# Routed experts on one core: where VectorE computes the remainders of the next block's weights

## The reference, cut to what matters

```python
logits = x @ gate_weight.T
scores = softmax(logits, axis=-1)
topk_w, topk_idx = top_k(scores, 2)
combine = zeros((T, E)).at[arange(T)[:, None], topk_idx].add(topk_w)
gu = einsum('th,efh->tef', x, gate_up_weights)      # E = 8, F = 352, H = 512
act = silu(gu[..., :F]) * gu[..., F:]
y = einsum('tef,te,ehf->th', act, combine, down_weights)
```

## Time and profile before

| | |
|---|---|
| time, median of 3 runs | 2822.68 us (2808.33, 2822.68, 2824.14) |
| the profiled execution's own time | 2808.16 us |
| its span | 2806.4 us |
| busy: PE, PEld | 2506.0 us (89%), 1464.9 us (52%) |
| busy: DVE, ACT, POOL | 1851.2 us (66%), 1257.6 us (45%), 1384.7 us (49%) |
| share of the chain that ended last | PE 52%, DVE 18%, POOL 10% |

### The profile page before, as it was taken

How to read it: one execution, slowest core, us unless ns; L and a number is a source line. 1 busy time by engine, 2 the same in 40 slices (tenths; PEclk the granted TensorE clock), 3 DMA queues, 4 the chain that set the end, 5 groups by cost and what they waited for, 6 DMA issues and landing times.

```text
span 2806.4 us, 33198 instructions
## 1 busy us (share of the span) xinstructions
PE 2506.0 (89%) x11722; PEld 1464.9 (52%) x11786; DVE 1851.2 (66%) x2240; ACT 1257.6 (45%) x1997; POOL 1384.7 (49%) x741
## 2 busy tenths in 40 slices
PE   5998949999999999989578799988988999999998
PEld 2454524444577888855233233333333333687776
DVE  4677875554565666556689789788978898722223
ACT  3443205541223666433557655763665443234333
POOL 0221338870050000330499999899999996122221
PEclk9999859998999999999899999999999999999999
DMA  6443583432053777531275676677576675100000
GB/s 222 139 120 101 78 120 87 95 86 113 12 226 133 261 260 261 197 116 51 94 196 153 179 203 176 162 192 205 168 196 195 166 209 194 57 0 16 15 1 30
DMA packets 278967, 384.98 MB, mean 137 GB/s; under 512 B 127104, under 2 KB 148608, under 8 KB 271392
## 3 DMA queue, kind: packets, MB, share of 16 engines
q1 hardware_dynamic: 268944, 335.77, 41.1%
q0 software_dynamic: 9296, 38.80, 5.6%
q10 hardware_dynamic: 576, 8.39, 0.7%
HBM read 312.91 MB, written 59.51 MB: 133 GB/s over the span
## 4 chain that ended last, share of the span: by engine, by line
PE 52%; DVE 18%; POOL 10%; issue 7%; ACT 5%; SPq 5%; DMA 3%; PEldq 0%; DVEq 0%; ACTq 0%; POOLq 0%; PEld 0%
PE psum L2037 7%; POOL arena L786 5%; PE psum L2215 4%; PE psum L2216 4%; POOL arena L792 4%; PE psum L1984 4%; SPq L2291 3%; DVE psum L1567 3%; DVE arena L1567 2%; PE psum L3017 2%; PE psum L2830 2%; PE psum L2188 2%; PE psum L2189 2%; DVE arena L2601 2%; PE psum L483 2%
## 5 line engine op out<-in xcount | busy, mean ns | idle before, releaser
L786 POOL TENSOR_TENSOR arena<-arena 128x1024 f32<-128x1024 f32 x256 | 625.8, 2453 | 137.8 <-DVE arena L1552 81.1
L2037 PE MATMUL psum<-arena,cst 128*128 128x512 f32 x1024 | 511.0, 638 | 118.5 <-POOL arena L792 87.2
L1090 ACT ACTIVATE psum<-arena,negA 128x512 f32<-128x512 f32 x512 | 333.3, 682 | 273.0 <-DVE arena L1567 234.1
L2037 PEld LDWEIGHTS psum<-arena,cst 128*128 128x128 f32 x1024 | 193.8, 201 | 422.4 <-issue 201.7
L1567 DVE TENSOR_TENSOR_SCAN arena<-psum,arena 128x512 f32<-128x512 f32 x256 | 310.7, 1213 | 101.3 <-ACT psum L1090 74.1
L1567 DVE TENSOR_TENSOR_SCAN psum<-psum,arena 128x512 f32<-128x512 f32 x256 | 297.9, 1209 | 37.3 <-POOL arena L786 36.4
L792 POOL TENSOR_TENSOR arena<-arena 128x1024 f32<-128x1024 f32 x128 | 308.0, 2407 | 10.9 <-DVE arena L1567 10.7
L840 POOL TENSOR_TENSOR arena<-arena 128x512 f32<-128x512 f32 x64 | 92.3, 1442 | 324.4 <-ACT arena L1215 299.4
L1984 PE MATMUL psum<-arena 128*128 128x512 f32 x512 | 230.3, 593 | 1.3 <-PE psum L1984 0.8
L2379 POOL TENSOR_TENSOR arena<-arena,cst 128x512 f32<-128x512 f32 x64 | 76.9, 1228 | 275.9 <-DVE arena L2683 191.4
L2367 POOL TENSOR_TENSOR arena<-arena,cst 128x1024 f32<-128x1024 f32 x96 | 184.7, 1952 | 43.0 <-PE psum L2931 25.7
(11 more groups left out here) (373 smaller groups left out, 4976.5 us busy)
## 6 DMA issues: line engine op xcount, KB each, us to landing
arena<-bc_scr SPq DMA_DIRECT2D x256, 512.0 KB, 5.5
arena<-w_exp SPq DMA_DIRECT2D x23, 1408.0 KB, 6.2
arena<-in_gu SPq DMA_DIRECT2D x48, 512.0 KB, 5.4
arena<-in_inw SPq DMA_DIRECT2D x32, 512.0 KB, 3.7
arena<-in_dn SPq DMA_DIRECT2D x31, 512.0 KB, 6.9
x_scr<-arena SPq DMA_DIRECT2D x19, 512.0 KB, 5.9
arena<-in_x SPq DMA_DIRECT2D x8, 1024.0 KB, 11.7
w_exp<-in_gu SPq DMA_DIRECT2D x16, 512.0 KB, 7.1
```

Of the source, the lines that this page charges most:

```text
L786: nc.gpsimd.tensor_tensor(dB[:, k % 4], du[:, j:j + 2], BC[:, k % RING, 0].unsqueeze(1).broadcast_to([P, 2, T]), ALU.mult).then_inc(s["db_ ...
L1090: nc.scalar.activation(psum[:, bank], dt[:, b % 2, j + t], ACT.Exp, scale=negA2[:, at:at + 1]).then_inc(s["da_ok"], 1)
L2037: ins = mm(psum[:, t], ident, dB[:, k % 4, t], start=False, stop=(n == NS - 1), skip_group_check=True)
```

## The change

`pieces(h)` now gives two lists, cut after the first `EARLY[h % 5]` pieces: two where h mod 5 = 0, otherwise one.

- VectorE: in front of `act_lo(h-1)` it does only the first list. The second list moves behind `tokens_lo(h+1)`; where h mod 5 = 4 it stays between `act_lo` and `act_b`.
- ScalarE: nothing changes but where h mod 5 = 3. There (3g+2, 2) moves from in front of `silu_b` to behind `act_hi`, and (3g+2, 3) from behind `act_hi` to behind `tokens_hi`.
- h = 0 stays as it was.

```diff
@@ ScalarE
-                if h:
-                    for k, j in pieces(h)[:-1]:
-                        hi(k, j)
+                first, then = pieces(h)
+                for k, j in first:
+                    hi(k, j)
                 silu_b(h)
                 if h:
                     act_hi(h - 1)
-                    for k, j in pieces(h)[-1:]:
+                    for k, j in then[:1]:
                         hi(k, j)
...
                     tokens_hi(h + 1)
-                if h == 0:
-                    for k, j in pieces(h):
-                        hi(k, j)
+                for k, j in then[1 if h else 0:]:
+                    hi(k, j)
                 if h:
                     rows_out(h - 1)
@@ VectorE
             for h in range(NH):
+                first, then = pieces(h)
+                for k, j in first:
+                    lo(k, j)
                 if h:
-                    for k, j in pieces(h)[:-1]:
-                        lo(k, j)
                     act_lo(h - 1)
-                    for k, j in pieces(h)[-1:]:
+                if h % 5 == 4:
+                    for k, j in then:
                         lo(k, j)
                 act_b(h)
                 if h + 1 < NH:
                     tokens_lo(h + 1)
-                if h == 0:
-                    for k, j in pieces(h):
+                if h % 5 != 4:
+                    for k, j in then:
                         lo(k, j)
@@ pieces
+        EARLY = (2, 1, 1, 1, 1)
+
         def pieces(h):
 
             at = [(3 * (h // 5) + k, j) for k, j in PIECE_AT[h % 5]]
-            return [(k, j) for k, j in at if 0 < k < NBLK]
+            cut = EARLY[h % 5] if h else 0
+            return [[(k, j) for k, j in part if 0 < k < NBLK] for part in (at[:cut], at[cut:])]
```

## The result

The changed kernel takes 2809.02 us in the median of 20 runs (2788.75 to 2822.12), the kernel before 2818.37 us in the median of its 20 runs beside them. The ratio is 0.997, with a 95% interval of 0.9956 to 0.9985; it leaves out one run of the kernel before, of 3673.78 us. That is about 8.5 us less (4.2 to 12.4), and the interval does not hold 1. The forecast was 7.8 us less and a median of 2814.9 us, in a range of 2797 to 2824.

What follows compares the result with a forecast made beforehand. TensorE was taken to set the pace, so only its pauses could be won: 5.6 us (gate) + 3.4 (down) - 1.2 (late load) = 7.8 us less, 2822.7 - 7.8 = 2814.9 us, range 2797 to 2824.

Steps and rivals of the forecast that it cites:

- What bounds the stage: Loop over the halves: TensorE, busy 34.43 of 35.00 us, sets the pace; only its pauses can be won.
- the ceiling of 21.6 us: TensorE's weight-load waits, 13.3 us at gate for `tokens_lo` and 8.3 at down for `act_lo`: the most to win.
- The price of a pause: On TensorE, a gate pause costs 0.40 us and a down pause 0.48, less at gate than the weight load's wait suggests.
- The sum of the parts: Over the loop: 5.6 us of gate pauses plus 3.4 of down pauses, less 1.2 for the load, gives 7.8 less.
- 14 x 0.40 = 5.6 us: Gate pauses at h mod 5 = 1 and 3 go when VectorE's last pieces move behind `tokens_lo`: 5.6 us won.
- 7 x 0.48 = 3.4 us: Seven down pauses at h mod 5 = 3 go, with one piece instead of two before `act_lo`: 3.4 us won.
- The cover of the moved pieces: VectorE's idle time before its next first piece, 2.70 us in the row, hides a moved piece, so `act_lo` is not delayed.
- The late load: Block 3g+4's load, issued later, makes ScalarE wait some 1.2 us in iteration 0, seven times: 1.2 us lost in all.
- by the sum: In iterations 0 and 1, with landing time L, ScalarE waits L - 6.52 us and a period loses L - 7.53.
- Slower by the late load: Rival: at a landing of 11.2 us, block 3g+4's load makes the kernel 17 us slower, 2839.7 us; chance 0.05.
- Nothing: Rival: the waits are a symptom of TensorE's own pace and the gaps stay, 2822.7 us; chance 0.07.
- most of it comes back: Rival: gate pauses at h mod 5 = 1 and iteration 3's late `act_lo` return; gain 2.8 us, 2819.9; chance 0.10.

Runs made afterwards that it cites:

- iteration 0 alone: Kernel before, with only VectorE's last piece of iteration 0 moved behind the tokens; loop from h = 3 took 252.7 us, against 255.5 before.
- iteration 3 as before: Changed kernel with the old order restored on both engines where h mod 5 = 3; loop from h = 3 took 252.9 us, against 247.5 changed.
- iteration 2 alone: Kernel before, with only VectorE's last piece of iteration 2 moved behind the tokens; loop from h = 3 took 255.8 us, against 255.5 before.
- iteration 3 alone: Kernel before, with the new order only where h mod 5 = 3, on both engines; loop from h = 3 took 256.0 us, against 255.5 before.
- the load still later: Changed kernel, with SyncE issuing block 3g+4's load only after VectorE's piece (3g+3, 0) too; loop from h = 3 took 265.7 us, against 247.5.

## Why the prediction was right, and where its steps were not

*What bounds the stage: right.* TensorE sets the pace, and with all its pauses gone the loop is shorter by 11.4 us from h = 3, within the ceiling of 21.6 us. Of the rest, 6.7 us are three waits that stay: 3.5 and 1.6 in the first halves, and 1.6 at the last down of the loop. The remaining 3.5 us are mostly waits that overstate their pause.

*The price of a pause: right.* 0.40 us at gate: iteration 0 alone brought 2.8 us in seven periods. The rule that an undisturbed weight load is early and a waiting load overstates the pause holds.

*The sum of the parts: right in total, wrong in how it is split.* The step that failed is "14 x 0.40 = 5.6 us" beside "7 x 0.48 = 3.4 us", as if the seven pauses at gate of 3 and the seven at down of 3 were separate. They are one delay. ScalarE's two pieces begin behind `rows_out`, which begins 0.43 us behind down's last matmul, whether gate has paused or not. `act_lo` is therefore ready at a fixed distance from the last down, and a gate that starts earlier only meets a longer pause at down. The same three places in the kernel before (last down, `act_lo`, first down of iteration 3, the last in the earlier trace rows too):

```profile
938.43 0.40 PE L1909 MATMUL psum<-r 96*128 96x512 f32 x1
```

```profile
943.43 0.55 DVE L1413 TENSOR_TENSOR r<-psum,r 128x384 fp32r<-128x384 f32 x1
```

`act_lo` ends 5.55 us behind that last down and down starts 5.61 behind it (944.04), with a gate pause between them. With iteration 3 as before and no gate pause they are 5.54 and 5.60 (941.30 and 941.36 less 935.76). Measured from h = 3: iteration 2 alone changed the loop by +0.4 us, iteration 3 alone won 0.50 us a period ahead of the late load, both together 0.88 (14.26 to 13.38). The prediction's 0.40 + 0.48 is the same 0.88, because it costed the state in which both are gone. Taken as the worth of each edit it misled, in the expectation of the kernel with iteration 3 as before. That the total came out is therefore no proof of its two terms.

*The cover of the moved pieces: right.* VectorE's next first piece was not late by a moved one; 0.93 and 0.28 us of idle time remained in the places shown above.

*The late load: mechanism right, size too large.* The issue came at 8.59 (8.65), ScalarE waited, and the wait reached gate by the sum to within 0.1 us. Mis-sized was the landing time: 7.7 us, the median of before, was taken for all seven. After, the trace has a landing for 11 of the 22 last DMAs, with a median of 7.1 us (6.4 to 9.3), and for three of the seven late loads: 8.08 in the period shown, and 6.87 and 6.94. ScalarE waited five times, 0.25, 1.42, 1.24 and 0.81 us and once about 0.2, not seven times 1.2. By the sum only 1.42 and 1.24 cost anything, 0.41 + 0.23; measured in iterations 0 and 1 of these two periods are 0.42 + 0.26, 0.7 us in the whole loop instead of 1.2. One addition in the prediction is off by 0.1 us: 6.1, 1.22 and 0.68 make 8.0 and not 7.9, which would have put the issue at 8.8.

The Trainium skill, DMA: Bandwidth & Descriptors, section on the anatomy of one DMA, gives 2.0 us plus bytes over 436 GB/s for one DMA that GpSimd issues. Used as an estimate for this load, which is three DMAs that SyncE issues, it makes 7.0 us and would have had no wait at all. The waits of 0.25 to 1.42 us speak against that use of it: the loads of the changed kernel whose landing the trace has took 8.0 to 10.4 us from the first issue to the last landing. Why they take longer no run here shows.

*The rivals.* "Slower by the late load" did not come, but the experiment with a later load shows that its mechanism is real: 2.5 us more, and the kernel's loop is 10 us longer than before. Its price of 26 us rested on a landing of 11.2 us, and that one belongs to a load of the first halves (issued at 883.11); the seven loads of block 3g+4 landed within 7.4 to 8.2 us before. "Nothing" and "most of it comes back" did not come. *The runs:* the time of the profiled execution was in neither place I expected (2820.65 us, where 2800.4 was forecast beside the one of before): a single whole time of this kernel cannot tell 8 us, but its loop can.

## What to carry to other kernels

Two pauses of the pacing engine within one round may be one delay seen twice: before adding their prices, ask whether the second one's deadline moves with the first, and price the edits together. Work that another engine must do can go into that engine's idle time behind the urgent step, but follow what it releases: here the last piece also released the next load. The gain survived where that load's piece stood behind the tokens' remainder, and was lost where it stood in front. Where one remaining piece is forced in front of a deadline, move the whole list ahead by one place, not the piece behind it.

## What the runs showed of the hardware

In these runs some longer pauses of TensorE were followed by a stretch at the lower clock, and so cost a second time. In the kernel with the load still later, gate of h = 11 started at 973.18, 2.23 us behind the last down matmul. The windows around it (length, busy of PE, PEld, DVE, ACT, POOL, then the granted clock, the DMA share and GB/s):

```profile
971.00:973.20 2.20, 0.36 (x3) 0.02 (x1) 0.77 (x2) 2.20 (x4) 0.00 (x0) 1.00 1.11 444
973.20:974.30 1.10, 1.10 (x6) 1.10 (x7) 1.10 (x1) 0.95 (x1) 0.00 (x0) 0.91 1.01 430
974.30:977.60 3.30, 3.30 (x14) 3.23 (x14) 1.99 (x3) 1.08 (x3) 0.00 (x0) 0.51 0.99 391
977.60:981.50 3.90, 3.90 (x23) 3.53 (x23) 2.21 (x4) 1.40 (x2) 0.00 (x0) 1.00 0.48 147
```

The clock was still full when the matmuls began again, and about a microsecond later it was at 0.51, the lower level of 1.2 GHz, while TensorE was busy without a gap. That cost iteration 1 about 1.6 us, and came in three of the seven periods (iteration 0 of 8.80, 8.75 and 8.58 us with it; 8.58, 8.30, 9.61 and 8.31 without). The length of the pause does not decide it: TensorE sat idle for 1.84, 1.79 and 1.60 us where the clock fell, and for 1.62, 1.32, 2.63 and 1.35 where it did not. In the changed kernel, whose pauses at gate are below 0.4 us, no iteration from h = 3 on shows it.

The first halves show such stretches too, the kernel before among them. There TensorE sits idle for 3.1 to 3.3 us ahead of down of the first half, which waits for `act_lo`, in each of the 13 profiled executions; in nine of the ten where the clock fell around it, it fell during this pause, and in one about a microsecond behind it. The changed kernel in its first profile, then in its second, the start of this down and a window around it:

```profile
904.28 0.80 PE L1911 MATMUL psum<-r 128*128 128x512 f32 x1 [3.26 <-DVE r L1412]
902.90:909.70 6.80, 5.42 (x14) 4.56 (x15) 3.53 (x6) 2.19 (x4) 0.00 (x0) 0.50 0.43 124
```

```profile
905.16 0.50 PE L1911 MATMUL psum<-r 128*128 128x512 f32 x1 [3.14 <-DVE r L1412]
904.50:911.30 6.80, 6.14 (x35) 5.74 (x36) 4.01 (x7) 3.29 (x6) 0.00 (x0) 1.00 0.45 121
```

After nearly the same pause the clock was at 0.50 in the one and full in the other, and from the gate of h = 0 to that of h = 2 they took 18.93 and 16.41 us. So it goes through all 13: the seven executions with a stretch at 0.50 as long as this took 18.4 to 18.9 us there, three with one half as long 17.3 to 17.8, and three with none 16.1 to 16.5. This is most of what one kernel's loops differ by. Which of two like pauses is followed by the lower clock no run here shows.
